# Layer 0's queries in three banks, a quarter of them issued a round early, and two multiplies moved ahead of a scan

## The chip, the cores and the metric

One core of one Trainium2 chip runs the whole program in one launch. Its engines are TensorE (PE in the rows), VectorE (DVE), ScalarE (ACT), GpSimd (POOL) and SyncE (SP), each with its own stream of instructions; DMA transfers run beside them. TensorE writes to PSUM, here eight banks of 128 partitions by 512 floats, PS0 to PS7. The metric is the device time of the program in microseconds, and lower is better.

## The reference

Two graph transformer layers on 3125 nodes with 128 features, 8 heads of 16 channels, and 53125 edges (25000 in either direction and one loop for each node), sorted by destination. Each layer adds its result to its input and normalises the sum. Cut to the core:

```python
# layer 0; layer 1 adds e = edge_attr @ We to k[src] and v[src],
# and takes x @ Wskip + bskip in place of the first residual;
# layer 0 counts one more loop for each node
h = layer_norm(x)
q, k, v = h @ Wq + bq, h @ Wk + bk, h @ Wv + bv        # 8 heads x 16
e = sum(q[dst] * k[src], axis=-1) / sqrt(16)
m = segment_max(e, dst)
p = exp(e - m[dst])
alpha = p / segment_sum(p, dst)[dst]
agg = segment_sum(alpha * v[src], dst)
x = x + agg @ Wo + bo
x = x + gelu(layer_norm(x) @ W1 + bf1) @ W2 + bf2
```

All arithmetic is float32.

## The kernel before

The nodes are 25 blocks (NB) of 128. The edges are padded to 26 batches (G) of 16 tiles (J) of 128 edges; a quarter of a batch is four tiles. Each layer has a node phase that makes queries QT (which stay in SBUF, by feature and node block) and a table of keys and values in HBM, then the edge loop of this study, then attention output and FFN over the node blocks.

The edge loop is a software pipeline written out by hand: on each engine a function `round(n)` is called for n = 0 to G + 1 and issues steps of the batches n + 1, n, n - 1 and n - 2. Nothing reorders them; an engine executes its stream in order, and engines meet through semaphores, each a counter. `done(name, n)` is a wait until the n-th signal of that name.

- **GpSimd**, `gather(n)`: 16 indirect DMAs of 128 rows (L487) fetch keys and values of the edges' sources into KV, one of four slots. A half of eight waits for agg_ready of the batch four earlier, which has the same slot: of its quarters 0 and 1 for the first half, 2 and 3 for the second. So in round n, while batch n is at work, batch n + 2 is fetched into the slot of batch n - 2.
- **TensorE** issues per round of layer 0: `add_up(n-2, 0)` and `(n-2, 1)`, four matmuls each (L828, banks PS4 and PS5), values by a matrix of positions OH; `queries_of(n, 2)`; `add_up(n-2, 2)`; `queries_of(n, 3)`; `add_up(n-2, 3)`; `queries_of(n+1, 0)`; `turn_alpha(n-1)` (L803) and `spread_gains(n-1)` (L807); `queries_of(n+1, 1)`; `turn_logits(n)` (L799), the transpose of the logits that the scan of the next round reads. A quarter of queries is eight float32 matmuls (L782 and L783, 16 records in the trace) of one-hots OHT by QT into PS0 or PS1, for four tiles: queries by edge. It waits for the product that last used its bank (prod_done, one quarter ahead), and for the one-hots. In layer 1 `edge_part` (L793) stands between.
- **VectorE**: `add_edges` waits for a gathered half and, in layer 1, adds the edge part (L1084). `products(n, q)` multiplies keys by the queries' bank (L1091) and signals prod_done; `add_products` sums each head's 16 channels to logits (L1098), l_ready. `forward_max(n-1)` is the scan of the batch's maxima (L954, FW) on the transposed logits and waits for lt_ready; `turn_max`, `backward_max`, `carry_max`, `max_back` and `shifts` (L1134 to L1137) finish the maximum of each destination. Then sums, `windows` (L1193, OH), `alphas` (L1178), `gains` (L1184), and `weigh` (L1203, four per batch), which scales the values and lets add_up go.
- **ScalarE**: `add_up` (L608, L612, L616) takes each quarter's sums out of PS4 or PS5 into AGG, and its act_col lets TensorE use the bank again; exp (L642), gates (L647, L648), one-hots for quarters 2 and 3 (L592, L595), and `scale_at_d` (L638), a copy for which turn_logits waits (rcs_ready).

The prefetch goes so far that the batches 0 to 3 are gathered without waiting. The last batch with logits, G - 1, has an order of its own on VectorE (`last_logits`).

## Time and profile before

| | us |
|---|---|
| median of three runs | 1723.95 |
| lowest, highest | 1722.98, 1724.45 |
| profiled execution | 1738.07 |
| its span | 1736.3 |

The profiled execution has a mean granted TensorE clock of 0.797 of full speed. Its rows in the section below give times in microseconds from the start of the span. In a timeline row the number in square brackets is how long the engine had been idle before this instruction, and, behind the arrow, what ended the wait; "remote" stands for a signal from elsewhere, a DMA mostly, and "issue" for nothing that the profile shows. The starts of matmuls are recorded, their ends are modelled. Register instructions and waits are not counted as busy. The loops of layer 0 and layer 1 lie at about 145 to 760 and 970 to 1640.

### The profile page before, as it was taken

The numbers are of one execution on the slowest core, as the hardware profiler recorded it, in microseconds if no ns is written. First come the engines' busy times: TensorE is split into PE (matmuls) and PEld (weight loads), VectorE is DVE, ScalarE is ACT, GpSimd is POOL, SyncE is SP. The second block draws the span as 40 slices with busy tenths as digits, with TensorE's granted clock in tenths as the row PEclk, the third lists the DMA queues.
The fourth block names the chain that finished last, engine by engine and source line by source line (L and its number), as shares of the span: only waits on it lengthen the run. The fifth ranks groups of instructions, "written<-read, shape, count | busy, mean of one in ns | idle before, by whom it ended". The sixth has DMA issues, their size and how long they took to land. (4 is left out here: it accounts for less than half of the span.)

```text
span 1736.3 us, 27275 instructions
## 1 busy us (share of the span) xinstructions
PE 1130.5 (65%) x6789; PEld 1009.3 (58%) x6789; DVE 1069.6 (62%) x2766; ACT 848.8 (49%) x2617; POOL 896.0 (52%) x1001
## 2 busy tenths in 40 slices
PE   4405657656656676769940577777776777777775
PEld 2305556656656566658830467666665666667674
DVE  5505565666656566775620566666666676766866
ACT  1203555555656465655410254555545455555775
POOL 3572666565656666303367065555655555553044
PEclk9756787787878877879975778787887887978888
DMA  5642455545544544420133255555555455444101
GB/s 164 140 123 86 127 152 160 153 125 156 159 140 139 162 153 128 147 75 17 45 117 104 89 157 160 158 151 161 154 156 161 141 165 155 155 147 139 65 2 38
DMA packets 100397, 222.63 MB, mean 128 GB/s; under 512 B 34859, under 2 KB 49482, under 8 KB 96669
## 3 DMA queue, kind: packets, MB, share of 16 engines
q0 software_dynamic: 39936, 109.11, 21.8%
q1 hardware_dynamic: 57511, 109.45, 19.9%
q10 hardware_dynamic: 2806, 2.38, 0.5%
q8 instruction: 62, 1.02, 0.2%
q14 instruction: 82, 0.67, 0.1%
HBM read 185.13 MB, written 35.74 MB: 127 GB/s over the span
## 5 line engine op out<-in xcount | busy, mean ns | idle before, releaser
L487 POOL DMA_INDIRECT KV<-kv_table,idx x832 | 802.2, 964 | 585.0 <-issue 457.3
L782 PE MATMUL PS<-QT,OHT 128*128 x1664 | 427.0, 346 | 321.5 <-DVE PR L1091 166.2
L782 PEld LDWEIGHTS PS<-QT,OHT 128*128 128x128 f32 x1664 | 336.2, 248 | 362.1 <-issue 360.3
L783 PE MATMUL PS<-QT,OHT 128*128 x1664 | 410.9, 336 | 17.7 <-issue 17.4
L783 PEld LDWEIGHTS PS<-QT,OHT 128*128 128x128 f32 x1664 | 338.2, 251 | 19.9 <-issue 19.9
L616 ACT ACTIVATE AGG<-AGG,PC,RCS x800 | 311.7, 390 | 2.2 <-ACT AGG L612 1.5
L1084 DVE TENSOR_TENSOR KV<-KV,PS 128x1024 f32<-128x1024 f32 x104 | 125.7, 1208 | 253.6 <-remote 191.9
L828 PE MATMUL PS<-OH,KV 128*128 128x128 f32 x1600 | 237.9, 293 | 63.5 <-issue 56.2
L608 ACT ACTIVATE PC<-PS 128x4 f32<-128x4 f32 x200 | 34.7, 174 | 493.3 <-PE PS L828 250.9
L828 PEld LDWEIGHTS PS<-OH,KV 128*128 128x128 f32 x1600 | 215.7, 208 | 66.9 <-issue 63.8
L1091 DVE TENSOR_TENSOR PR<-KV,PS 128x512 f32<-128x512 f32 x208 | 140.8, 677 | 179.2 <-issue 80.4
L612 ACT ACTIVATE AGG<-PS 128x127 f32 x800 | 209.7, 262 | 1.0 <-issue 0.7
L592 ACT ACTIVATE OHT<-REL,minus_part 128x1024 f32<-128x1024 bf16 x104 | 113.3, 1136 | 143.6 <-remote 139.9
L1203 DVE TENSOR_TENSOR KV<-KV,PS 128x512 f32<-128x512 f32 x208 | 128.7, 680 | 29.5 <-remote 29.2
L1098 DVE TENSOR_REDUCE Ls<-PR 128x32 f32<-128x512 f32 x208 | 139.6, 671 | 0.4
L496 POOL TENSOR_TENSOR ROOT<-VAR,minus_half 128x4 f32<-128x4 f32 (+1 forms) x35 | 33.4, 955 | 184.2 <-DVE VAR L1349 184.2
L793 PE MATMUL PS<-We,EA 128*128 128x256 f32 x416 | 119.2, 422 | 5.5 <-issue 5.3
L595 ACT ACTIVATE OHT<-OHT,one_col 128x1024 f32<-128x1024 f32 x104 | 113.2, 1136 | 0.0
L793 PEld LDWEIGHTS PS<-We,EA 128*128 128x128 f32 x416 | 82.6, 214 | 17.9 <-issue 8.8
L803 PE MATMUL PS<-ident,AL 128*128 128x128 f32 x52 | 21.3, 409 | 104.7 <-DVE AL L1178 85.9
L954 DVE TENSOR_TENSOR_SCAN FW<-GA,PS 128x128 f32<-128x128 bf16 x52 | 21.7, 416 | 92.5 <-issue 86.5
L1073 DVE TENSOR_SCALAR OHT<-REL,iota_part 128x1024 f32<-128x1024 bf16 x104 | 77.6, 748 | 0.0
(173 smaller groups left out, 1340.0 us busy)
## 6 DMA issues: line engine op xcount, KB each, us to landing
REL<-rel_dram SPq DMA_DIRECT2D x52, 512.0 KB
window_dram<-OH SPq DMA_DIRECT2D x25, 1024.0 KB
OH<-window_dram SPq DMA_DIRECT2D x50, 512.0 KB
KV<-kv_table,idx POOLq DMA_INDIRECT x832
EA<-in_edge_batch SPq DMA_DIRECT2D x52, 256.0 KB
kv_table<-KV SPq DMA_DIRECT2D x50, 128.0 KB, 1.7
GATES<-edge_gates SPq DMA_DIRECT2D x8, 208.0 KB
window_dram<-KV SPq DMA_DIRECT2D x1, 1024.0 KB
```

The source lines that it names most:

```text
L487: g.indirect_dma_start(KV[:, s, j, :], None, kv_table, bass.IndirectOffsetOnAxis(ap=idx[:, s, j:j + 1], axis=0)).then_inc(gathered[s][hh], 16)
L592: sc.activation(OHT[:, 1, nf, :], REL[:, 8 * P:16 * P], ACT.Abs, bias=minus_part[:, nf:nf + 1]).then_inc(S["oht2_step"], 1)
L612: sc.activation(AGG[:, ds(at + 1, P - 1)], bank[:, m, 1:P], ACT.Copy).then_inc(S["act_col"], 1)
L616: sc.activation(AGG[:, ds(at, 1)], AGG[:, ds(at, 1)], ACT.Identity, bias=PC[:, m:m + 1], scale=RCS[:, n % SLOTS, j:j + 1]).then_inc(S["act ...
L782: te.matmul(o, OHT[:, q // 2, 0, e0:e0 + P], QT[:, ds(blk, P)], start=True, stop=False)
L783: last = te.matmul(o, OHT[:, q // 2, 1, e0:e0 + P], QT[:, ds(blk + P, P)], start=False, stop=True)
L793: last = te.matmul(PS[2 + q % 2][:, 2 * m * D:2 * (m + 1) * D], EA[:, e0:e0 + P], We[:, :], start=True, stop=True)
L828: last = te.matmul(PS[4 + q % 2][:, m * P:(m + 1) * P], KV[:, n % SLOTS, j, D:2 * D], at[:, j * P:(j + 1) * P], start=True, stop=True)
L1084: v.tensor_tensor(kv, kv, ep, ALU.add).then_inc(S["e_used"], 1)
L1091: v.tensor_tensor(PR[:, q % 2, :].rearrange("p (j d) -> p j d", j=4), KV[:, n % SLOTS, 4 * q:4 * q + 4, 0:D], PS[q % 2][:, :].rearrange("p ...
L1098: v.tensor_reduce(Ls[:, :].rearrange("p (h j) -> p j h", h=H)[:, 4 * q:4 * q + 4, :], PR[:, q % 2, :].rearrange("p (j h c) -> p j h c", j= ...
L1203: v.tensor_tensor(v4, v4, at, ALU.mult).then_inc(S["pv_ready"], 1)
```

## The change

Three things change, in the orders written by hand; the counts of all computing instructions stay.

- `query_banks`: the quarters of layer 0's queries take PS0, PS1 and PS3 in turn, by (4n + q) mod 3, where before they took PS0 and PS1. `queries_of` then waits for the product three quarters back and no longer two. Layer 1 keeps two banks.
- TensorE, layer 0: `queries_of(n+1, 2)` stands at the end of round n, behind `turn_logits(n)`, and no longer in round n + 1 behind its first two quarters of `add_up`. For batch 0 it stands ahead of the rounds.
- VectorE, both layers: `products(n, 0)`, `add_edges(n, 1)` and `products(n, 1)` stand ahead of `forward_max(n-1)`; `add_products(n, 1)` stands ahead of `shifts(n-1)`.

```diff
--- before.py
+++ after.py
@@ -178,6 +178,7 @@
         gain_at_d = PS[6][:, P:P + J]
         iota_psum = PS[2][:, 0:P]
         logits_t, alpha_t = PS[6][:, 0:P], PS[7][:, 0:P]
+        query_banks = [[PS[0], PS[1], PS[3]], [PS[0], PS[1]]]
         attention_of, turned2_of, ffn_of, turned_of = PS[0], PS[1][:, 0:P], PS[6][:, 0:P], PS[7][:, 0:P]
 
         S = {n: sem(n) for n in """x_loaded x2_loaded dst_loaded dste_loaded gates_in first_weights weights_loaded
@@ -774,10 +775,11 @@
                     if q % 2 == 0:
                         blks[:] = values(block_row, n * J + 4 * q, 8, ENG.PE, NP - P)
                         pe.wait_ge(*done("oht2_ready" if q // 2 else "oht_ready", n * 2 + (2 * G * l + 2)))
-                    pe.wait_ge(*done("prod_done", n * 4 + (4 * G * l + q - 1)))
+                    banks = query_banks[l]
+                    pe.wait_ge(*done("prod_done", n * 4 + (4 * G * l + q + 1 - len(banks))))
                     for m in range(4):
                         blk = blks[q % 2 * 4 + m]
-                        o = PS[q % 2][:, m * P:(m + 1) * P]
+                        o = banks[(4 * n + q) % len(banks)][:, m * P:(m + 1) * P]
                         e0 = ((4 * q + m) % 8) * P
                         te.matmul(o, OHT[:, q // 2, 0, e0:e0 + P], QT[:, ds(blk, P)], start=True, stop=False)
                         last = te.matmul(o, OHT[:, q // 2, 1, e0:e0 + P], QT[:, ds(blk + P, P)], start=False, stop=True)
@@ -864,7 +866,7 @@
                         return
                     if n == G:
                         turn_logits(n - 1)
-                    if logits:
+                    if logits and l:
                         queries_of(n, 2)
                     if sums:
                         add_up(n - 2, 2)
@@ -888,9 +890,13 @@
                             edge_part(n + 1, 1)
                     if logits and n < G - 1:
                         turn_logits(n)
+                    if more and l == 0:
+                        queries_of(n + 1, 2)
 
                 queries_of(0, 0)
                 queries_of(0, 1)
+                if l == 0:
+                    queries_of(0, 2)
                 if l:
                     edge_part(0, 0)
                     edge_part(0, 1)
@@ -1089,7 +1095,7 @@
                     dve.wait_ge(*done("qe_ready", n * 4 + (4 * G * l + q + 1)))
                     dve.wait_ge(*done("l_ready", n * 4 + (4 * G * l + q - 1)))
                     v.tensor_tensor(PR[:, q % 2, :].rearrange("p (j d) -> p j d", j=4), KV[:, n % SLOTS, 4 * q:4 * q + 4, 0:D],
-                                    PS[q % 2][:, :].rearrange("p (j d) -> p j d", j=4), ALU.mult).then_inc(S["prod_done"], 1)
+                                    query_banks[l][(4 * n + q) % len(query_banks[l])][:, :].rearrange("p (j d) -> p j d", j=4), ALU.mult).then_inc(S["prod_done"], 1)
 
                 def add_products(n, q):
                     dve.wait_ge(*done("prod_done", n * 4 + (4 * G * l + q + 1)))
@@ -1211,25 +1217,22 @@
                         return
                     if logits:
                         add_edges(n, 0)
+                        products(n, 0)
+                        add_edges(n, 1)
+                        products(n, 1)
                     if soft:
                         forward_max(n - 1)
-                    if logits:
-                        products(n, 0)
-                    if soft:
                         turn_max(n - 1)
                         backward_max(n - 1)
                         carry_max(n - 1)
                     if logits:
-                        add_edges(n, 1)
                         add_products(n, 0)
                     if soft:
                         max_back(n - 1)
                     if logits:
-                        products(n, 1)
+                        add_products(n, 1)
                     if soft:
                         shifts(n - 1)
-                    if logits:
-                        add_products(n, 1)
                     places = one_hots1(n + 1) if more else iter(())
                     next(places, None)
                     if logits:
```

TensorE, layer 0, the seam of two rounds. Before, the transpose of the logits (PS6) is followed by add_up's quarters 0 and 1 (PS4, PS5) and then by the load of a block index and the queries of quarter 2, of which the first rows stand here:

```order
L799 MATMUL PS6<-ident,Ls 128x128 [waits rcs_ready,l_ready]
L828 MATMUL PS4<-OH,KV 128x128 [waits act_col,pv_ready,oh_ready]
L828 MATMUL PS4<-OH,KV 128x128 x3
L828 MATMUL PS5<-OH,KV 128x128 [waits act_col,pv_ready]
L828 MATMUL PS5<-OH,KV 128x128 x3
L202 TENSOR_LOAD block_row
L782 ISA [waits prod_done,oht2_ready]
L782 MATMUL PS0<-QT,OHT 128x128
```

The same seam after the change, first how it begins:

```order
L801 MATMUL PS6<-ident,Ls 128x128 [waits rcs_ready,l_ready]
L203 TENSOR_LOAD block_row
L784 ISA [waits prod_done,oht2_ready]
L784 MATMUL PS3<-QT,OHT 128x128
L785 ISA
L785 MATMUL PS3<-QT,OHT 128x128
```

and, behind the eight matmuls of that quarter, how it goes on:

```order
L830 MATMUL PS4<-OH,KV 128x128 [waits act_col,pv_ready,oh_ready]
L830 MATMUL PS4<-OH,KV 128x128 x3
L830 MATMUL PS5<-OH,KV 128x128 [waits act_col,pv_ready]
L830 MATMUL PS5<-OH,KV 128x128 x3
L830 MATMUL PS4<-OH,KV 128x128 [waits act_col,pv_ready,oh_ready]
L830 MATMUL PS4<-OH,KV 128x128 x3
L784 ISA [waits prod_done]
L784 MATMUL PS0<-QT,OHT 128x128
```

The load and the quarter of queries went from behind to ahead of add_up's first two quarters, and the third quarter of add_up follows these two at once.

VectorE, layer 0, where a round begins behind the last multiply of the values (L1203, L1209). Before:

```order
L1203 TENSOR_TENSOR KV<-KV,PS7 128x4x128 x3
L954 SCALAR_TENSOR_TENSOR FW<-GA,PS6 128x128 [waits ga_ready,lt_ready,gathered20]
L1091 TENSOR_TENSOR PR<-KV,PS0 128x512 [waits l_ready,qe_ready]
L1119 STREAM_TRANSPOSE max_row<-FW 128x2x16 [waits max_kept,fwd_done]
L954 SCALAR_TENSOR_TENSOR MX<-GA,FW 128x128 [waits fwd_done]
L954 SCALAR_TENSOR_TENSOR mrow<-gates,max_row 128x34 [waits max_turned,gate_loaded]
L1098 TENSOR_REDUCE Ls<-PR 128x4x8 [waits lt_ready,prod_done]
L1128 STREAM_TRANSPOSE max_before<-mrow 128x32 [waits carry_row]
L1129 COPY max_row<-mrow 128x2
L1091 TENSOR_TENSOR PR<-KV,PS1 128x512 [waits l_ready,qe_ready]
L1134 SCALAR_TENSOR_TENSOR MX<-GF,max_before,MX 128x128 [waits bwd_done,max_back]
```

After:

```order
L1209 TENSOR_TENSOR KV<-KV,PS7 128x4x128 x3
L1097 TENSOR_TENSOR PR<-KV,PS3 128x512 [waits l_ready,qe_ready,gathered20]
L1097 TENSOR_TENSOR PR<-KV,PS0 128x512 [waits l_ready,qe_ready]
L960 SCALAR_TENSOR_TENSOR FW<-GA,PS6 128x128 [waits ga_ready,lt_ready]
L1125 STREAM_TRANSPOSE max_row<-FW 128x2x16 [waits max_kept,fwd_done]
L960 SCALAR_TENSOR_TENSOR MX<-GA,FW 128x128 [waits fwd_done]
L960 SCALAR_TENSOR_TENSOR mrow<-gates,max_row 128x34 [waits max_turned,gate_loaded]
L1104 TENSOR_REDUCE Ls<-PR 128x4x8 [waits lt_ready,prod_done]
L1134 STREAM_TRANSPOSE max_before<-mrow 128x32 [waits carry_row]
L1135 COPY max_row<-mrow 128x2
L1104 TENSOR_REDUCE Ls<-PR 128x4x8 [waits prod_done]
L1140 SCALAR_TENSOR_TENSOR MX<-GF,max_before,MX 128x128 [waits bwd_done,max_back]
```

Both multiplies of keys by queries (L1091, now L1097) now stand ahead of the scan of the maxima (FW), the second one by nine rows, and the second sum of products ahead of the shifts (L1134, now L1140).

## Rows read from the trace of the kernel before

**Rows 1.** The page: head.
```profile
span 1736.3 us, 27275 instructions
```

**Rows 2.** The table by stretches: us, busy PE, PEld, DVE, ACT, POOL, then clock.
```profile
145.00:720.00 575.00, 379.07 (x2295) 348.02 (x2294) 369.68 (x897) 317.45 (x978) 339.10 (x352) 0.79 0.47 144
```

**Rows 3.** One line's instructions, 190 to 722: count, ns min/median/max, first and last start.
```profile
L954 DVE TENSOR_TENSOR_SCAN FW<-GA,PS x22: 419/421/421, 192.8 to 721.0; 128x128 f32<-128x128 bf16 x22
```

**Rows 4.** Timeline, GpSimd: start, us, line, op, tiles, count, [idle before <-releaser].
```profile
407.91 0.95 POOL L487 DMA_INDIRECT KV<-kv_table,idx  x1 [2.49 <-remote]
...
420.36 0.94 POOL L487 DMA_INDIRECT KV<-kv_table,idx  x1 [2.73 <-issue]
...
432.96 0.94 POOL L487 DMA_INDIRECT KV<-kv_table,idx  x1 [2.79 <-remote]
```

**Rows 5.** Groups by line, 150 to 720: count, busy, mean ns, idle before, releasers.
```profile
L487 POOL DMA_INDIRECT KV<-kv_table,idx x352 | 339.1, 963 | 239.7 <-issue 183.7 <-remote 47.6 <-PE PS L828 8.4
...
L782 PE MATMUL PS<-QT,OHT 128*128 x736 | 191.2, 348 | 79.9 <-DVE PR L1091 51.9 <-issue 24.4 <-DVE OHT L1073 3.1
...
L1091 DVE TENSOR_TENSOR PR<-KV,PS 128x512 f32<-128x512 f32 x92 | 62.1, 675 | 106.8 <-issue 63.1 <-remote 36.1 <-PE PS L783 7.5
```

**Rows 6.** Timeline, TensorE, layer 0.
```profile
214.43 2.01 PE L828 MATMUL PS<-OH,KV 128*128 128x128 f32 x16
...
391.17 3.36 PE L828 MATMUL PS<-OH,KV 128*128 128x128 f32 x16
...
416.04 2.01 PE L828 MATMUL PS<-OH,KV 128*128 128x128 f32 x16
...
420.71 0.48 PE L782 MATMUL PS<-QT,OHT 128*128 x2 [2.66 <-DVE PR L1091]
...
422.59 1.06 PE L828 MATMUL PS<-OH,KV 128*128 128x128 f32 x8
...
431.16 1.25 PE L782 MATMUL PS<-QT,OHT 128*128 x2 [1.12 <-issue]
...
434.76 0.64 PE L783 MATMUL PS<-QT,OHT 128*128 x2
...
692.49 2.01 PE L828 MATMUL PS<-OH,KV 128*128 128x128 f32 x16
```

**Rows 7.** Timeline, ScalarE, layer 0.
```profile
406.89 0.17 ACT L608 ACTIVATE PC<-PS 128x4 f32<-128x4 f32 x1 [7.00 <-remote]
...
415.59 0.16 ACT L638 ACTIVATE RCS<-PS 128x16 f32<-128x16 f32 x1
...
419.50 0.17 ACT L608 ACTIVATE PC<-PS 128x4 f32<-128x4 f32 x1 [3.75 <-PE PS L828]
...
431.94 0.17 ACT L608 ACTIVATE PC<-PS 128x4 f32<-128x4 f32 x1 [6.91 <-remote]
```

**Rows 8.** Timeline, VectorE, layer 0.
```profile
419.47 0.42 DVE L954 TENSOR_TENSOR_SCAN FW<-GA,PS 128x128 f32<-128x128 bf16 x1 [4.17 <-issue]
...
429.03 0.69 DVE L1091 TENSOR_TENSOR PR<-KV,PS 128x512 f32<-128x512 f32 x1 [4.68 <-issue]
```

**Rows 9.** Timeline, all engines, when GpSimd's gathers of layer 0 are over.
```profile
725.38 1.40 PE L828 MATMUL PS<-OH,KV 128*128 128x128 f32 x8
...
726.81 0.17 ACT L608 ACTIVATE PC<-PS 128x4 f32<-128x4 f32 x1 [0.39 <-PE PS L828]
```

**Rows 10.** Timeline, GpSimd, start of layer 0's loop.
```profile
168.91 0.95 POOL L487 DMA_INDIRECT KV<-kv_table,idx  x1 [28.63 <-issue]
```

**Rows 11.** Timeline, VectorE, end of layer 0's loop.
```profile
720.97 0.42 DVE L954 TENSOR_TENSOR_SCAN FW<-GA,PS 128x128 f32<-128x128 bf16 x1 [4.19 <-issue]
```

**Rows 12.** Timeline, VectorE, GpSimd and TensorE, a round of layer 1.
```profile
1458.35 0.41 DVE L954 TENSOR_TENSOR_SCAN FW<-GA,PS 128x128 f32<-128x128 bf16 x1
...
1458.44 0.95 POOL L487 DMA_INDIRECT KV<-kv_table,idx  x1 [5.30 <-issue]
...
1459.59 0.48 PE L782 MATMUL PS<-QT,OHT 128*128 x2 [1.95 <-DVE PR L1091]
```

## The prediction

> **What bounds the kernel now.** I read the page first: a span of 1736.3 us [rows 1]. The table by stretches shows the edge loop of layer 0, of 575 us, with TensorE busy for 379, VectorE for 370, ScalarE for 317 and GpSimd for 339, at a mean granted clock of 0.79 [rows 2]. No engine is full, so the bound is a loop of waits or something that busy shares don't show.
>
> Then I looked for a beat. The scan of the maxima, once a round, stands at 192.8 and at 721.0, with 22 instances [rows 3]: 21 rounds of 25.15 us. Which engine keeps it? In GpSimd's timeline it issues eight gathers, waits, issues eight more, waits. Halves begin at 407.91, 420.36 and 432.96, and the waits ahead of them are 2.49, 2.73 and 2.79 us [rows 4]. So a half is 12.5 us, some 9.7 of issuing and 2.75 of waiting. In the loop 352 gathers are busy for 339.1 us with 239.7 idle [rows 5]: less the one long pause of 28.63 [rows 10] and less seven gaps of 0.30 in each of 44 halves (92), that is 2.75 us for each half, so few can be much shorter. GpSimd waits there for add_up: the first half of a round's gathers for quarters 0 and 1 of the batch two rounds back, the second half for quarters 2 and 3.
>
> What ends that wait? At 416.04 the sixteen matmuls of add_up's quarters 0 and 1 start, and they are modelled as finished at 418.05 [rows 6]. Yet ScalarE, which wants the first eight of them, starts at 419.50 after 3.75 us idle [rows 7], VectorE's scan, which wants the transpose ahead of them, at 419.47 [rows 8], and GpSimd goes on at 420.36 [rows 4]. The same in the next half: the queries of quarter 2 (from 420.71) are through by 422.59, when add_up's quarter 2 starts, which ends at 423.65 [rows 6]. But VectorE multiplies that quarter of queries at 429.03, after 4.68 us idle [rows 8], and ScalarE takes up that quarter of sums at 431.94, after 6.91 us [rows 7]. Compare the end of the layer, when GpSimd has no gather left: eight matmuls of add_up run from 725.38 to 726.78, and ScalarE follows at 726.81, after 0.39 us [rows 9]. So while gathers are under way, what TensorE has finished by its rows is seen late, in one burst some 1.8 us behind GpSimd's last issue (420.36 - 2.73 = 417.63, and the burst at 419.5). My reading: the beat is 9.7 us of issuing, 1.8 until the burst and 0.9 until GpSimd goes on, and the work of TensorE and VectorE only has to be there before the burst. Waits shortened inside a half change nothing unless they move the burst.
>
> The Trainium skill, "SBUF — State Buffer", section "SBUF: two separate sides", speaks against this reading: engine ports and DMA ports are disjoint, a DMA can't slow a compute engine, and TensorE waits for no one. By that rule the late starts would be real waits in a chain, and the change, which removes two of them, would pay in full (rival D). The pair of 423.65 and 431.94 disagrees with it, unless something else than a port holds the signals, which no row tells.
>
> **The change, part by part.** Instruction counts stay. The sum is made on the profiled execution, 1738.07 us, and carried as a difference to the median of the runs, 1723.95.
>
> 1. VectorE, both layers: the products of quarters 0 and 1 move ahead of the scan. In layer 0 they fill a wait: 4.17 us ahead of the scan [rows 8], against 2 x 0.675 = 1.35 us of work (62.1 us over 92 [rows 5]). VectorE is then 1.35 us earlier behind the burst; that is off the path: 0. The condition is that the queries of both quarters are seen before the burst. Else the scan stands behind a waiting product, and the shifts and ScalarE's exp behind that; since both are seen with the burst at the latest, the cost would be at most 1.35 us a round. I take 0, as both are multiplied a half earlier.
>
> 2. TensorE, layer 0: the queries of quarter 2 go behind turn_logits, ahead of add_up's quarters 0 and 1. A quarter takes 1.9 us at full clock (420.71 to 422.59) and 4.2 at half clock (431.16 to 435.40) [rows 6]. That pushes back exactly the add_up that GpSimd waits for, so this term decides. Slack at 416.04 is 418.05 to 419.5, 1.45 us. It grows by what comes earlier: turn_logits stands behind ScalarE's copy at 415.59, which follows, with the one-hots between, on add_up's quarters 2 and 3 from 406.89, taken there after 7.00 us idle [rows 7]. With its queries gone from the front of the round, quarter 2 of add_up stands 1.9 us earlier in TensorE's row, and is seen in the first half if signals of that time still get through, as ScalarE's take-up at 419.50 did. Then the copy is earlier by up to one quarter of ScalarE's work, 2.4 us, at least by 0; I take 2.0, nearer to the first, as ScalarE is idle for 6.91 us just there. Full clock: 1.9 against 2.0 + 1.45, cost 0. Half clock: at 391.17 the sixteen took 3.36 us, with nothing to spare before the next half, so the cost is 4.2 - 2.0 = 2.2. The loop has 20 such rows (the first at 214.43, the last at 692.49 [rows 6]): 12 of about 2.0 us, 6 between 2.2 and 2.6, two of 3.4 to 3.5. So 2 x 2.2, and 6 x 0.15 for the mixed ones (2.9 us of queries, between the two prices, against 3.2 of room that is itself unsure): 5.3 us, +0.25 a round.
>
> 3. The next round's first half loses that work from its front: add_up's quarters 2 and 3, for which GpSimd's second half waits 2.79 us [rows 4], are 1.9 us earlier in TensorE's queue. The wait ends with the burst, so this is worth between 0 and some tenths; I take -0.2, as quarter 3 comes first in the burst. With step 2: +0.05 x 21 = +1.
>
> 4. The third bank makes step 2 possible and lifts TensorE's waits for VectorE's products (51.9 us ahead of L782 [rows 5]). They lie within a half: 0. If the halves were not what bounds, this would be up to -2.5 us a round (51.9 over 21), which is rival D.
>
> 5. Start and end of layer 0. GpSimd pauses once for 28.63 us, until 168.91 [rows 10], for add_up's first quarters. One more quarter of queries stands ahead of them: +1.9, less 1.0 for the earlier VectorE. Bounds +1.9 and -6 (if signals of a quarter move forward by a half of such a round, 12.5 / 2, in the same backlog); I take +1. At the end the scan at 720.97 waits 4.19 us [rows 11], into which the products fit: -0.6, at most -1.35.
>
> 6. Layer 1 keeps two banks and TensorE's order. Its GpSimd waits 5.30 us at 1458.44, beside a scan at 1458.35 that has no wait of its own, and TensorE's queries at 1459.59 waited 1.95 us for the first product [rows 12], which is now ahead of the scan: 0.3 us earlier (0.41 of the scan, less overlap). The scan, the shifts and exp come 1.3 us later, by the two products. What is behind exp, the sums, is not what GpSimd waits for in that half. Bounds -0.3 and +0.6 us (half of the 1.3, if exp becomes the chain) in 22 rounds: -7 and +13. I take 0, as the two effects touch waits that end for other reasons.
>
> Sum: +1 (rounds), +1 (start), -0.6 (end), 0 (layer 1) = +1.4: 1739.5 in such an execution, 1725.3 as the median; I say 1725.
>
> **Rivals.**
> B, slower: the added queries overrun the burst, in the last half of each round of layer 0, behind turn_logits. It decides from the point where add_up's second quarter ends later than 11.6 us behind the half's start (419.5 - 407.91). With nothing gained on ScalarE: 1.9 - 1.45 = 0.45 us in 12 rounds, 2.9 - 1.2 = 1.7 in 6, 4.2 in 2, together 24, with the start 1750. With half of the gain (1 us): 0, 6 x 0.7 and 2 x 3.2 = 10.6, and 1.9 at the start: 1736, the value I give it. For it: the mean clock of 0.79 and nothing to spare at 391.17. Against it: 1.45 us of slack in the rounds at full clock.
>
> C, a little faster: GpSimd's second half goes on sooner, because add_up's quarters 2 and 3 are seen before the burst. Of the 2.79 us I give it 0.6: 21 x 0.6 = 13, 1711. For it: quarter 2 of add_up moves to where signals still got through. Against it: the mean of 2.75 us over all halves, in many of which the work was long done.
>
> D, clearly faster: the late starts are real waits of a chain. VectorE's idle ahead of the products is 106.8 us in the loop [rows 5]; if half of it went, as the queries of two quarters in four come earlier, 53 us, 1671. Against it: 422.59 and 429.03, with VectorE idle between.
>
> E, no effect: both moves fall inside hidden time in every round: 1724. It is told apart from the forecast by the profile alone.
>
> **How the numbers follow.** Forecast with E 0.42, B 0.31, C 0.20, D 0.07. A measurement of this kernel tells 0.2%, 3.4 us, from no change: faster is below 1720.5, slower above 1727.4. The forecast's own spread (layer 1, the start) puts 0.34 within, 0.03 below, 0.05 above; B puts 0.01 within and 0.30 above; C 0.01 within and 0.19 below; D 0.07 below. Faster 0.29, same 0.36, slower 0.35. The range leaves out D, the upper quarter of B (0.08) and a quarter of C (0.05): 1708 to 1742. The forecast's own range is 1719 to 1732, with the bounds of layer 1 and start taken at half.
>
> **What the changed profile would show.** Step 1: the scan's wait falls from 4.2 to some 2.8 us behind two products, and the beat stays at 25.1 to 25.2. Step 2: in a round at full clock the sixteen matmuls of add_up end less than 11.6 us behind the half's start, and ScalarE's copy stands 2 us earlier in its half. Step 3: ScalarE takes quarter 2 in the first half, quarter 3 with the burst, and GpSimd's waits stay near 2.75. Step 5: the pause ends 1 us later. Step 6: the beat of layer 1 stays. I am wrong if GpSimd's waits in layer 0 fall below 2 us in many halves (C, D: the burst is no law) or rise above 3 (B), or if the later scan delays add_up in layer 1.

## The result: 1756.0 us, slower, outside the forecast range

| | median us | runs | ratio to before | 95% interval |
|---|---|---|---|---|
| before | 1724.2 | 4 | | |
| after | 1756.0 (1751.4 to 1762.0) | 4 | 1.0182 | 1.0147 to 1.0216 |

The change costs 1.8%, 32 us. The forecast was 1725, from 1708 to 1742. The profiled execution of after took 1752.28 us. That of before, 1738.07, was a long one of its kind, so the two traces differ by only 14 us, and what they differ by has to be read stage by stage. Here is the scan of the maxima (FW, once a round), with count, duration in ns, first and last start: first of before in the last rounds of layer 0 (its loop stands in [rows 3]), then of after, in the loop and in the last rounds:

```profile
L954 DVE TENSOR_TENSOR_SCAN FW<-GA,PS x2: 409/411/413, 736.9 to 754.3; 128x128 f32<-128x128 bf16 x2
```

```profile
L960 DVE TENSOR_TENSOR_SCAN FW<-GA,PS x21: 412/414/421, 195.9 to 717.1; 128x128 f32<-128x128 bf16 x21
...
L960 DVE TENSOR_TENSOR_SCAN FW<-GA,PS x3: 414/415/420, 743.9 to 780.5; 128x128 f32<-128x128 bf16 x3
```

Before, the scan of round 23 is at 721.0 [rows 3] and the last one at 754.3. After, they are at 743.9 and 780.5. So layer 0 loses 26 us: 23 of them inside the loop, which the prediction had put at +1, and some 3 behind it. The loss isn't spread over the rounds. The timeline of GpSimd in after (start, duration, line, operation, [idle before]) has here the first gathers of five halves, and one gather inside a half (251.96):

```profile
200.13 0.95 POOL L488 DMA_INDIRECT KV<-kv_table,idx  x1 [10.31 <-issue]
...
237.19 0.95 POOL L488 DMA_INDIRECT KV<-kv_table,idx  x1 [2.18 <-remote]
...
249.88 0.95 POOL L488 DMA_INDIRECT KV<-kv_table,idx  x1 [2.96 <-issue]
...
251.96 1.05 POOL L488 DMA_INDIRECT KV<-kv_table,idx  x1 [1.13 <-issue]
...
261.36 0.95 POOL L488 DMA_INDIRECT KV<-kv_table,idx  x1 [0.50 <-issue]
...
281.62 0.95 POOL L488 DMA_INDIRECT KV<-kv_table,idx  x1 [10.53 <-issue]
```

Most halves are as before: 12.2 to 13.1 us from their first gather to the next half's, with 1.9 to 3.4 us of waiting. But the half that begins at 249.88 has only 0.50 us of waiting behind it, and lasts 11.5 us. The one behind it waits 10.53 us and lasts 20.3. There are four such pairs in the loop (10.7 and 20.0, 11.5 and 20.3, 11.2 and 20.4, 11.3 and 20.0; the waits at 200.13 and 281.62 end the first two). Against 12.4 the long ones cost 31 us and the short ones give 5 back: 26 us, of which the other halves return some 4. That is the loss in the loop. Three of the four short halves are among the five that have a gap of 1.13 us at their second gather, as at 251.96; why these were hit wasn't followed. In the trace of before, whose like halves stand in [rows 4], none is longer than 13.2 us.

What happens in such a pair, on all engines of after (PE TensorE, DVE VectorE, ACT ScalarE):

```profile
255.49 1.14 PE L830 MATMUL PS<-OH,KV 128*128 128x128 f32 x8
...
263.63 0.48 PE L805 MATMUL PS<-ident,AL 128*128 128x128 f32 x1 [5.22 <-DVE AL L1184]
...
273.44 2.48 DVE L1209 TENSOR_TENSOR KV<-KV,PS 128x512 f32<-128x512 f32 x4 [7.74 <-remote]
...
273.48 0.18 ACT L639 ACTIVATE RCS<-PS 128x16 f32<-128x16 f32 x1 [6.48 <-remote]
...
274.68 0.79 PE L784 MATMUL PS<-QT,OHT 128*128 x2 [0.42 <-issue]
...
278.25 2.57 PE L830 MATMUL PS<-OH,KV 128*128 128x128 f32 x16
...
279.96 0.17 ACT L609 ACTIVATE PC<-PS 128x4 f32<-128x4 f32 x1 [6.30 <-PE PS L830]
```

And the like places of an ordinary pair of halves in the trace of before:

```profile
429.67 0.37 PE L828 MATMUL PS<-OH,KV 128*128 128x128 f32 x1 [1.16 <-issue]
...
435.90 0.33 PE L803 MATMUL PS<-ident,AL 128*128 128x128 f32 x1 [0.51 <-DVE AL L1178]
...
437.88 2.47 DVE L1203 TENSOR_TENSOR KV<-KV,PS 128x512 f32<-128x512 f32 x4
```

Read them in this order. Add_up's quarter 3 is through at 256.6, 6.8 us behind the half's start at 249.88; before, its last matmul (429.67) ends 9.7 us behind the start at 420.36 [rows 4]. So in after this quarter is seen when GpSimd's last issue ends, and GpSimd goes on without a pause. The transpose of alpha is issued 2.3 us later, at 263.63, into a stream of gathers that has had no gap. VectorE, which waits for it, gets it at 273.44, after 7.74 us idle, and ScalarE gets the gains' product, 273.48 after 6.48 us. In before GpSimd pauses from 430.2 to 432.96, the transpose at 435.90 comes 2.9 us behind the start of the half, and VectorE uses it at 437.88. My reading, still to be tested: the pause that the prediction counted as waiting is what lets the second hop of the round through. Without it the hop waits for the next burst, and everything behind it (the weighing, turn_logits, add_up's first quarters, GpSimd's next half) starts a half too late. And only there the added queries count in full: they run from 274.68 to 278.25, 3.6 us at a granted clock of 0.50, ahead of the sixteen matmuls that GpSimd waits for.

I call this the theory of the missed burst (M). The rivals in the experiments are O, that the added queries overrun in every round (the prediction's B), and V, that VectorE's new order is the cause.

### The profile page after: what moved, and what is told of

Read it like the earlier page. It is cut to its first block and busy times, and to the rows that moved or that the text cites. A ratio compares the mean times of both kernels' runs of the same rounds, so it can differ in the third digit from the quotient of the medians.

```text
span 1750.5 us, 27275 instructions
## 1 busy us (share of the span) xinstructions
PE 1120.0 (64%) x6789; PEld 1009.4 (58%) x6789; DVE 1084.3 (62%) x2766; ACT 842.9 (48%) x2617; POOL 900.7 (51%) x1001
## 5 line engine op out<-in xcount | busy, mean ns | idle before, releaser
L830 PE MATMUL PS<-OH,KV 128*128 128x128 f32 x1600 | 234.1, 294 | 79.1 <-ACT AGG L617 44.3
L1097 DVE TENSOR_TENSOR PR<-KV,PS 128x512 f32<-128x512 f32 x208 | 141.9, 685 | 205.4 <-remote 126.8
L1209 DVE TENSOR_TENSOR KV<-KV,PS 128x512 f32<-128x512 f32 x208 | 128.7, 680 | 37.5 <-remote 37.3
L805 PEld LDWEIGHTS PS<-ident,AL 128*128 128x128 f32 x52 | 8.7, 168 | 193.8 <-DVE AL L1184 176.9
L795 PEld LDWEIGHTS PS<-We,EA 128*128 128x128 f32 x416 | 80.7, 210 | 20.0 <-issue 11.3
```

The source lines that it names most:

```text
L795: last = te.matmul(PS[2 + q % 2][:, 2 * m * D:2 * (m + 1) * D], EA[:, e0:e0 + P], We[:, :], start=True, stop=True)
L830: last = te.matmul(PS[4 + q % 2][:, m * P:(m + 1) * P], KV[:, n % SLOTS, j, D:2 * D], at[:, j * P:(j + 1) * P], start=True, stop=True)
L1097: v.tensor_tensor(PR[:, q % 2, :].rearrange("p (j d) -> p j d", j=4), KV[:, n % SLOTS, 4 * q:4 * q + 4, 0:D], query_banks[l][(4 * n + q) % ...
L1209: v.tensor_tensor(v4, v4, at, ALU.mult).then_inc(S["pv_ready"], 1)
```

## The experiments

The single kernels did not all run on the same chip, and that turned out to matter. On some chips the kernel before takes 1724 to 1742 us, as in the runs above; on others it takes 1375 to 1376. I call them chips of the first and of the second kind. Each ratio is to runs of the kernel before on the same chip. M below stands for the missed burst, O for the overrun, V for VectorE.

### VectorE's order alone, TensorE's order alone, layer 1 alone (e1, e2, e3, second kind; e8, e9, first kind)

e1 and e9 keep this part of the change in layer 0 and undo the rest:

```diff
+                    if l == 0:
                         add_edges(n, 0)
                         products(n, 0)
                         add_edges(n, 1)
                         products(n, 1)
                         forward_max(n - 1)
...
+                    else:
+                        # the order of before
...
-        query_banks = [[PS[0], PS[1], PS[3]], [PS[0], PS[1]]]
+        query_banks = [[PS[0], PS[1]], [PS[0], PS[1]]]
...
-                    if logits and l:
+                    if logits:
                         queries_of(n, 2)
...
-                    if more and l == 0:
-                        queries_of(n + 1, 2)
```

e2 and e8 keep the banks and TensorE's order and take VectorE's order of before in both layers. e3 keeps VectorE's order in layer 1 alone.

> The kernel before, with only VectorE's new order, and that only in layer 0 (two banks, TensorE's order and layer 1 as before). Theory M (missed burst): the loss of the changed kernel comes from halves in which GpSimd goes on without its pause, because add_up's third and fourth quarters are seen early; these stand where they stood, so no half of 20 us appears, layer 0 keeps 25.1 us a round and the time is 1724 to 1728. Theory O (overrun): the queries ahead of add_up cost some time in each round; not in this kernel, 1724. Theory V (VectorE): the scan behind two multiplies delays the chain of the maximum by 1.35 us in each round of layer 0: 1724 + 30 = 1754.

> The kernel before with three banks and the queries of quarter 2 ahead of add_up in layer 0, VectorE's order as before in both layers. Theory M: four or five halves of 20 us behind a half of 11 to 11.7, rounds with them some 6 us longer, 1744 to 1756. Theory O: the same total, but spread as about 1 us over every round of layer 0, no half of 20 us. Theory V: 1724.

> The kernel before, with VectorE's new order in layer 1 alone. Between the two profiles layer 1 (scan of round 0 to the last) went from 659 to 644 us. If VectorE's order did that, this kernel takes 1709 to 1715 us; if the profiled execution of before was only a long one of its kind (1738 against a median of 1724), it takes 1722 to 1730.

> The kernel before with three banks and the early queries in layer 0 alone, VectorE's order as before. Where before takes 1724: theory M: halves of 20 us as in the changed kernel, 1744 to 1752, since it is TensorE's order that lets add_up's later quarters be seen early. If VectorE's order is needed for that as well: 1720 to 1730. Where before takes 1376: 1379 again.

> The kernel before with VectorE's new order in layer 0 alone. Where before takes 1724: theory M: no more halves of 17 to 20 us than in the kernel before (0 and 2 in its two traces), 1720 to 1730; theory V (the scan behind two multiplies sets the loss): 1750. Where before takes 1376: 1375 again.

| | kind | us | before there | ratio | interval |
|---|---|---|---|---|---|
| e1 VectorE, layer 0 | second | 1375.2 | 1376.1 | 0.9981 | 0.9966 to 0.9996 |
| e2 TensorE, layer 0 | second | 1378.9 | 1376.1 | 1.0017 | 1.0002 to 1.0031 |
| e3 VectorE, layer 1 | second | 1382.7 | 1376.1 | 1.0052 | 1.0037 to 1.0067 |
| e8 TensorE, layer 0 | first | 1754.8 | 1727.9 | 1.0111 | 1.0028 to 1.0193 |
| e9 VectorE, layer 0 | first | 1722.2 | 1727.9 | 0.9964 | 0.9941 to 0.9988 |

The first three could not test M: their chip knows no such halves. e3 asked whether VectorE's order had made layer 1 shorter in the trace of after; on this chip it makes the kernel 7 us longer. On the first kind TensorE's order alone brings a loss: 27 us by the medians, 19 us (5 to 33) by the ratio, which leaves out the longest run; the whole change lost 32 and, in e5 below, 27. (M had said 1744 to 1752; the median is 3 us above it.) VectorE's order alone is a gain of 6 us. Three of e8's four runs took 1753 to 1760 us and one 1731, so the loss differs much from one execution to the next; M would put that down to the number of missed bursts, but only the run of 1760 has a trace. GpSimd in it, one pair (11.1 us, then 21.0; the trace has four of 20.4 to 21.1 and one of 17.4), and then the end of one long half in e9:

```profile
246.22 0.94 POOL L488 DMA_INDIRECT KV<-kv_table,idx  x1 [3.44 <-issue]
...
278.36 0.95 POOL L488 DMA_INDIRECT KV<-kv_table,idx  x1 [11.32 <-issue]
```

```profile
275.98 0.94 POOL L488 DMA_INDIRECT KV<-kv_table,idx  x1 [7.49 <-issue]
```

e9 has two such halves, of 17.5 and 17.2 us, and none of 20. So it can miss a burst too, but each costs 3 us less. V falls.

### The kernel before and the changed kernel again (e5, e6, first kind; e15, second kind)

No edit.

> The changed kernel itself, once more. The first experiments ran where the kernel before takes 1376 us, and not 1724: there GpSimd issues its gathers of layer 0 without a pause, 16 x 1.25 = 20.0 us of a 20.4 us round. Theory M (missed burst) then says that the change does nothing in layer 0 there, as GpSimd's issuing is the bound: within 0.3% of the kernel before, 1372 to 1381, with the -1 us of VectorE's order in layer 0, +3 of the early queries and +6 of layer 1 as single parts add up to at most +8 (1384). Theory O (overrun) says that the added 1.9 us ahead of add_up are paid here too: 1376 + 21 x 1 = 1397 or more. If it runs where the kernel before takes 1724: 1751 to 1762 again, with four or five halves of 20 us.

> The kernel before itself, for a second trace of it. Where it takes 1376: GpSimd's gathers follow each other in 1.25 us in both layers, a round of layer 0 is 20.4 us, and what TensorE finishes is taken up within 0.5 us. Where it takes 1724: halves of 12.5 us in layer 0, and layer 1 some 14 us shorter than the 658.6 us (scans from 974.2 to 1632.8) of the first trace, which was 14 us above the median.

> The changed kernel, once more. Where the kernel before takes 1376, GpSimd's issuing is the bound of layer 0, and the parts measured there (VectorE in layer 0 -1, TensorE +3, VectorE in layer 1 +6) add up to +8: 1380 to 1388. Theory O (every round pays the added queries): 1397 or more. Where before takes 1724: 1747 to 1762 again.

e5: 1752.5 against 1726.0, ratio 1.0147 (1.0098 to 1.0197), with four halves of 20.1 to 21.0. e6: 1722.5. Its layer 1, from first to last scan, took 645 us against 659 in the first trace of before, which accounts for the 14 us by which that trace was long. This trace of before shows the missed burst too, twice (17.3 and 17.4 us). One of them:

```profile
255.10 0.94 POOL L487 DMA_INDIRECT KV<-kv_table,idx  x1 [0.48 <-issue]
...
257.38 0.47 PE L803 MATMUL PS<-ident,AL 128*128 128x128 f32 x1 [5.74 <-DVE AL L1178]
...
267.11 2.48 DVE L1203 TENSOR_TENSOR KV<-KV,PS 128x512 f32<-128x512 f32 x4 [7.67 <-remote]
...
267.90 3.75 PE L828 MATMUL PS<-OH,KV 128*128 128x128 f32 x16
...
272.45 1.01 POOL L487 DMA_INDIRECT KV<-kv_table,idx  x1 [7.64 <-issue]
```

GpSimd goes on after 0.48 us at 255.10, the transpose of alpha is issued at 257.38 and used at 267.11, after 7.67 us. But here the sixteen matmuls of add_up follow at 267.90 at once, and GpSimd waits 7.64 and not 10.53 us. The difference to after, 20.3 against 17.3 us, is the added quarter of queries in its place. So a missed burst is nothing new. The change makes it more frequent (four in either trace, in place of none and two) and each dearer by 3 us. What two of them cost doesn't show in the total of layer 0: from batch 4 on, 43 halves take 540.6 us in this trace and 540.5 in the first one, as the other halves here are 12.4 us and not 12.6. With the change the same 43 take 562.6 us (after) and 564.7 (e5).

e15, on the second kind: 1383.8 against 1374.9, ratio 1.0071 (1.0054 to 1.0088), inside M's 1380 to 1388 and far from O's 1397. GpSimd's gathers there follow each other (283 gathers from 200 to 560, 274.1 us busy and 86.2 idle, 0.30 for each):

```profile
L488 POOL DMA_INDIRECT KV<-kv_table,idx x283 | 274.1, 969 | 86.2 <-issue 86.2
```

### The pause forced back (e4, second kind; e7, first kind)

```diff
                     for hh in range(2):
                         pool.wait_ge(*done("agg_ready", ...))
+                        if l == 0 and hh:
+                            pool.wait_ge(gathered[s][0], u * 128)
                         pool.sem_inc(S["pool_go"], 1)
```

> The changed kernel, and in layer 0 GpSimd's second half of a batch's gathers waits until the first half has landed, which is when it went on before, some 2.7 us behind its last issue. Theory M: the pause comes back, the halves of 20 us go, layer 0 takes 25.0 to 25.2 us a round again and the time falls by 22 to 30 us, to 1726 to 1734. Theories O and V: the added work is still there and one more wait, so the time is 1756 or more.

> The changed kernel with GpSimd's second half of gathers in layer 0 waiting until the first half has landed, once more, for the case that the kernel before takes 1724 us. Theory M (missed burst): in the changed kernel four or five halves of 20 us follow a half of 10.7 to 11.5; with the pause forced back no half is under 12.2 and none 20, the rounds of layer 0 take 25.0 to 25.5 us and the time falls by 15 to 25 us, to 1729 to 1737. Theory O (overrun of the queries ahead of add_up): the extra time is in every round, nothing gets better: 1752 or more. If it runs where the kernel before takes 1376: 1458 as in the first experiment of this kind.

e7: 1731.3 us against 1727.9, ratio 1.0019 (0.9990 to 1.0048). One more wait in the changed kernel makes it 21 to 25 us faster than the changed kernel was on the two other chips of this kind, and equal to the kernel before. M had said 1729 to 1737, O 1752 or more. But not all of this is missed bursts. The wait acts on batches 0 to 3 as well, and there it lets the first gather of batch 4 start at 158.9 us and not at 169.4: 10.5 us that the kernel before doesn't have. The 43 halves behind it, where the missed bursts were, take 545.0 us, against 562.6 and 564.7 in the two traces of the changed kernel and 540.5 in the one of before: 18 to 20 of the 22 to 24 us lost come back, and 4.5 stay. No half of its loop is under 12.3 or over 14 us:

```profile
234.69 0.94 POOL L490 DMA_INDIRECT KV<-kv_table,idx  x1 [2.77 <-issue]
...
247.72 0.94 POOL L490 DMA_INDIRECT KV<-kv_table,idx  x1 [2.50 <-DMA KV<-kv_table,idx]
...
260.17 1.37 POOL L490 DMA_INDIRECT KV<-kv_table,idx  x1 [2.76 <-issue]
...
715.14 0.42 DVE L962 TENSOR_TENSOR_SCAN FW<-GA,PS 128x128 f32<-128x128 bf16 x1 [0.70 <-remote]
```

The same half that was 11.5 us and followed by 20.3 is now 13.0 (from 234.69), followed by 12.5, and the scan of round 23 is at 715.1 and not at 743.9. This wait ends when transfers have landed, so the experiment doesn't tell a pause in the issuing from one in the transfers. e4, the same kernel on the second kind, took 1458.7 us against 1376.1, ratio 1.0592 (1.0564 to 1.0621): where results aren't held, the pause is pure loss, as O and V had said of it everywhere.

### Nearly no gathers (e10, first kind; e16, second kind)

The edit, on the kernel before (e10) and on the changed one (e16); the waits count accordingly. Seven of eight gathers are left out in layer 0 from batch 4 on, so KV holds there what older batches left.

```diff
-                        for j in range(hh * 8, hh * 8 + 8):
+                        for j in range(hh * 8, hh * 8 + gathers_of(l, n)):
...
+        gathers_of = lambda l, n: 1 if l == 0 and n >= SLOTS else 8
```

> The kernel before with one gather per half in place of eight, in layer 0 from batch 4 on (the rest of KV keeps what older batches left in it, so this part of the sums is left out). It measures the disputed hold by itself. If the gathers hold back what TensorE has finished, ScalarE and VectorE follow its rows within 0.5 us in layer 0, and a round falls from 25.1 us to that of the chain of work, 15 to 20 us, in either place. If the late starts have another cause, the waits of 4 to 7 us stay and a round takes 23 us or more where before takes 1724.

> The changed kernel with one gather per half in place of eight in layer 0 from batch 4 on (that part of the gathering is left out). The kernel before took 16.5 us a round like this, 362.8 us from the scan of round 1 to that of round 23, with VectorE busy throughout. If the change has no cost of its own on the chain of work, 16.4 to 16.6 us a round here too, 360 to 365 us; if the added 1.9 us ahead of add_up are on it, 17 us or more, 375 us.

From the trace of e10: the scans, the table by stretches (columns as in [rows 2]) and a piece of the timeline.

```profile
L957 DVE TENSOR_TENSOR_SCAN FW<-GA,PS x23: 414/416/421, 184.7 to 546.9; 128x128 f32<-128x128 bf16 x23
...
200.00:500.00 300.00, 243.18 (x1822) 230.57 (x1820) 289.49 (x713) 252.37 (x799) 34.10 (x36) 0.91 0.37 116
...
347.74 0.30 PE L802 MATMUL PS<-ident,Ls 128*128 128x128 f32 x1 [0.47 <-ACT RCS L641]
...
347.87 2.01 PE L831 MATMUL PS<-OH,KV 128*128 128x128 f32 x16
...
349.03 0.17 ACT L611 ACTIVATE PC<-PS 128x4 f32<-128x4 f32 x1 [1.44 <-PE PS L831]
```

e10: 1537.8 us. On a chip of the first kind the same work now takes 16.5 us a round (362.2 us over 22) in place of 25.1, with VectorE busy for 289 of 300 us. ScalarE takes up add_up's first quarter at 349.03, 1.2 us behind its start and after 1.44 us idle, where it had waited 3.75 [rows 7]. So it is the stream of gathers that holds results back, or something that comes with it. The late starts, with their waits of 4 to 7 us, are gone.

e16, the changed kernel in the same form (1349.0 us, one run, on a chip of the second kind):

```profile
L963 DVE TENSOR_TENSOR_SCAN FW<-GA,PS x20: 408/410/419, 193.4 to 547.5; 128x128 f32<-128x128 bf16 x20
...
342.25 0.27 PE L804 MATMUL PS<-ident,Ls 128*128 128x128 f32 x1
...
344.29 1.95 PE L833 MATMUL PS<-OH,KV 128*128 128x128 f32 x16
...
345.39 0.17 ACT L612 ACTIVATE PC<-PS 128x4 f32<-128x4 f32 x1 [4.00 <-PE PS L833]
```

354.1 us over 19 rounds, 18.6 a round. My expectation of 360 to 365 for 22 rounds was wrong, and the other side of it, 17 us or more a round, is right. TensorE starts turn_logits at 342.25, and add_up's first two quarters 2.04 us later, not 0.13; ScalarE is idle for 4.00 us and not 1.44. A round is 2.2 us longer than in e10. (The two kernels ran on different kinds of chips, and e16 has VectorE's new order as well; neither was tested apart.) Layer 0's last round shows the added queries bare on the first kind, as its gathers are over there: first after, then before.

```profile
758.04 0.30 PE L801 MATMUL PS<-ident,Ls 128*128 128x128 f32 x1 [0.72 <-ACT RCS L639]
...
759.76 0.48 PE L784 MATMUL PS<-QT,OHT 128*128 x2 [1.42 <-issue]
...
762.39 2.83 PE L830 MATMUL PS<-OH,KV 128*128 128x128 f32 x16
```

```profile
736.14 0.30 PE L799 MATMUL PS<-ident,Ls 128*128 128x128 f32 x1 [0.89 <-ACT RCS L638]
736.28 2.01 PE L828 MATMUL PS<-OH,KV 128*128 128x128 f32 x16
```

Add_up starts 4.35 us behind turn_logits and not 0.14: 2.6 us of queries, and 1.42 of "issue" ahead of them, where the load of the block indices now stands (that the gap is this load is likely, not shown). The last two scans lie 21.5 us apart in every trace of the first kind with TensorE's new order (after, e5, e7, e8) and 17.4 in those without it (both of before, e9, e17, e18). So the added queries stand on the chain of work and cost 2 to 4 us a round when nothing covers them. O's place was right; what covers most of it seems to be GpSimd's issuing on the second kind and the burst on the first, except in the missed halves.

### Three banks without the early queries (e12, e14, second kind; e17, first kind)

The changed kernel, with queries_of(n, 2) put back in its old place and the third bank and VectorE's order kept.

> The changed kernel with its three banks and VectorE's new order in both layers, but TensorE's order of before (the queries of quarter 2 behind add_up's first two quarters). Theory M with the reordering of TensorE as its cause: halves of at most 17.5 us, none to two of them, 1720 to 1730 where before takes 1724 to 1728. If the third bank alone (queries let go one quarter earlier) makes the later quarters seen early: 1745 to 1755. Where before takes 1376: 1375 to 1384, as its parts.

> Three banks and VectorE's order, TensorE's order of before, once more. Where before takes 1724: theory M with the reordering of TensorE as its cause says 1720 to 1730 and halves of at most 17.5 us; if the third bank alone is the cause 1745 to 1755, with halves of 17 to 18 us but not of 20, as the added queries do not stand ahead of add_up. Where before takes 1376: 1382 again.

> Three banks and VectorE's order with TensorE's order of before. Where the kernel before takes 1724 to 1728: 1720 to 1730 with at most two halves of 17 us, if TensorE's order is the cause of the missed bursts; 1745 to 1755 if the third bank alone is. Where before takes 1376 it is 1382 a third time.

e17: 1736.6 against 1741.5, ratio 0.9971 (0.9959 to 0.9984), with one half of 17.5 us in its trace. So the third bank alone doesn't bring the loss; the order does. e12 and e14: 1382.1 and 1382.2, ratios 1.0039 (1.0024 to 1.0055) and 1.0057 (1.0039 to 1.0075). That is about what VectorE's order in layer 1 costs by itself (e3). Over the 22 rounds from its first scan, layer 1 takes 456.0 us in e1 (order of before) and 462.9 in e15, 0.3 us a round (first e1, then e15; e3, on e1's chip, takes 463.1):

```profile
L955 DVE TENSOR_TENSOR_SCAN FW<-GA,PS x23: 411/413/415, 755.9 to 1211.9; 128x128 f32<-128x128 bf16 x23
...
L960 DVE TENSOR_TENSOR_SCAN FW<-GA,PS x23: 410/412/414, 756.5 to 1219.4; 128x128 f32<-128x128 bf16 x23
```

### A pause in the start alone (e11, e13, second kind; e18, first kind)

The kernel of e9 with the pause of e7 for the batches 0 to 3 only.

> VectorE's new order in layer 0 alone (two banks, TensorE's order of before), and GpSimd's second half of gathers waits for the first to land for the batches 0 to 3 only. In the kernel before their 64 gathers run without a pause and TensorE's results wait until 149 us; with all halves paused the scan of round 3 stood at 206.1 in place of 217.9, but later rounds lost 6 us of that. Theory M: bursts in the start alone give most of these 12 us: 1727 - 5 (VectorE's order) - 10 = 1710 to 1716 where before takes 1724 to 1728. If the start is not what later rounds are counted from: 1722. Where before takes 1376 there is nothing to let out, and the pauses cost up to 9 us: 1376 to 1385.

> The kernel of the start pause once more, for the case that the kernel before takes 1724: theory M says 1710 to 1716, the scan of round 3 at 206 and not 218, and the later rounds as before. Where before takes 1376: 1390 again.

> VectorE's order in layer 0 and the pause in the first four batches only. Where the kernel before takes 1724 to 1728: 1710 to 1716, with the scan of round 3 at 206 and not 218. Where before takes 1376: 1390 a third time.

```profile
109.63 0.41 DVE L957 TENSOR_TENSOR_SCAN FW<-GA,PS 128x128 f32<-128x128 bf16 x1
...
211.80 0.41 DVE L957 TENSOR_TENSOR_SCAN FW<-GA,PS 128x128 f32<-128x128 bf16 x1
```

e18: 1735.2 against 1741.5, ratio 0.9962 (0.9947 to 0.9976). The first scan comes at 109.6 and not near 150, but the scan of round 3 only at 211.8, against 217.9 in both traces of before. Of 40 us 6 are left at that point, and the ratio is no better than that of e9, whose order of VectorE this kernel has too. The 8 to 18 us under the kernel before that I had expected were too much: it is 6, and it can't be said that the pause gives anything here. On the second kind the pauses cost 14 and 16 us (1390.3, 1.0095 with 1.0075 to 1.0115, and 1391.3, 1.0122 with 1.0102 to 1.0142), more than the 9 that I had allowed.

No kernel here is much better than before. The one that is ahead on both kinds is VectorE's order in layer 0 alone: 0.9964 (e9) and 0.9981 (e1), both less than half a per cent.

## Why the prediction was wrong, step by step

- **The bound.** Confirmed: GpSimd's halves keep the beat of layer 0, results of TensorE are held while gathers run (e10), and rival D, which took the late starts for real waits of a chain, had no case. The Trainium skill's rule behind it ("SBUF — State Buffer", section "SBUF: two separate sides", disjoint ports for engines and DMA) doesn't foretell the waits of the first kind, and the measurement decides; whether a port has to do with them no run here shows. The step that failed is the sentence that the work of TensorE and VectorE "only has to be there before the burst". A round has two hops in a row through TensorE: add_up's later quarters free the second half, and the transpose of alpha, in the second half, leads to the first quarters of the next round. That the pause between the halves gives the second hop its time to get through could have been asked of the trace of before (issued 2.9 us behind the start of a half, used at 437.88), but I had not followed that hop. The runs showed it in its place: where the pause is gone the second half takes 20.0 to 20.4 us (20.1 to 21.0 in e5), and with the pause forced back none does (e7).
- **Step 1, VectorE in layer 0.** Taken as 0; e9 and e1 gave -6 and -1 us. It was underrated and harmless.
- **Step 2, the queries ahead of add_up.** The price of a quarter was right (1.9 us at full clock and 3.6 to 4.2 at half). Its cost was placed in the wrong rounds: in the missed halves it is 3 us each, and in the last round 4.2 with the load of the block indices, for which the sum had no term. In ordinary rounds it is small. There the mean half is 12.49 us in after and 12.57 in the first trace of before, but on one and the same chip 12.52 against 12.40 (e5, e6) and 12.54 against 12.37 (e8, e9), so some 0.3 us a round, near the +0.25 of the sum. With one trace of each kernel that may be chance.
- **Step 3, quarters 2 and 3 of add_up come earlier.** The step that decided the result. It was put at 0 to -0.2 a round and in rival C at -0.6, a gain in either case. Seen earlier they were: GpSimd's wait fell from 2.8 to between 0.3 and 0.5 us in four halves, 5 us gained in all. But what followed cost 31 us. I had looked at what a shorter wait gives and not at what the wait was good for.
- **Rival B** had the right sign and the nearest sum (1736, with an upper end of 1750), by the wrong mechanism in the main: e7 keeps all its added work and gives 18 to 20 of the 22 to 24 us back, and in e15, where GpSimd's issuing is the bound, none of O's 21 us shows. The 4.5 us that stay in e7 can be B's. My own test of it, waits above 3 us in many halves, did not hold: there are four of some 10.5 us.
- **Step 4, the third bank**: 0, confirmed by e17. **Step 5**: the pause ended at 169.4, 0.4 us later, where +1 was forecast, and the end of the layer got worse by 3 us and not better by 0.6: no gathers cover the added queries of the last round, and its scan comes 4 us late. **Step 6, layer 1**: 0 with bounds -7 and +13; on the second kind it is +7 us, in which e3 and e15 agree. On the first kind the two traces of before differ by 14 us there, and nothing of this size can be told.
- **The range** had its upper end at 1742, since I had bounded each term of the rounds by what it costs where it stands and none by a step of the loop, a half.

## What to carry to other kernels

When two engines run in lockstep through a wait, ask what the wait lets through before shortening it: an engine that issues transfers and no longer pauses can take away the gap in which others' results got by. Follow every hop of a round through the held resource, not only the next one. And if a loop moves in steps of a whole half, bound each unknown by such a step, not by its own length.

## What the runs showed of the hardware

- The same program takes 1724 to 1742 us on chips of one kind (three in the experiments) and 1375 to 1376 on three others. On the latter gathers follow each other with no more than 0.30 us between them, the results of TensorE are used soon (in e15 add_up's first quarters start at 340.97 and ScalarE takes them up at 342.06), and a round of layer 0 takes 20.4 us (16 issues of 1.25 are 20.0). What differs between the chips isn't visible in these profiles and stays open.
- On the first kind, what TensorE finishes within some 3 us behind a pause of the gathers is seen within 2 us (435.90 and 437.88); what it finishes in a stream that had no pause is seen up to 9.3 us later (264.1 and 273.44). With one gather in eight the effect is gone (e10: 1.2 us from add_up's start to ScalarE). Why a stream of gathers has this effect was not found.
